# Clustered attention: the stacks are transposed by DMAs from SBUF to SBUF instead of PE and ACT, the softmax shift is one f16 part made on ACT, and the cluster sums are halved twice on POOL

## What is computed

```
x  = layernorm(inputs)
q, k, v = x @ Wq, x @ Wk, x @ Wv                       # per head 8 features
qb = softmax(q @ Whq);  kb = softmax(k @ Whk)          # per head 32 clusters
logits = q @ k.T / sqrt(8) + 0.1 * (qb @ kb.T)
out = (softmax(logits) @ v) @ Wo
```

## Time and profile before

| | |
|---|---|
| median of 3 runs | 1725.93 us (1725.49 to 1727.14) |
| profiled execution | 1726.9 us, its span 1725.1 us |
| PE busy in the span | 1432.3 us (83%) |
| DVE busy | 1264.7 us (73%) |
| ACT busy | 971.7 us (56%) |
| POOL busy | 859.6 us (50%) |
| row maxima on DVE, L656 | 256 x 1216 ns = 311.4 us |
| exponentials on ACT, L703 | 256 x 1028 ns = 263.2 us |
| copies of the stacks on ACT, L724 | 128 x 1028 ns = 131.2 us |
| transposes of the stacks on PE, L555 | 1024 x 228 ns = 83.4 us |

### The profile page before, as it was taken

One profiled execution on the slowest core, in us unless ns is written; L12 is line 12 of the kernel. 1 busy time (PEld: TensorE's weight loads), 2 busy tenths in 40 slices (PEclk: granted clock), 3 DMA queues, 4 the chain that ended last, 5 costly groups with the idle time before them and its releaser, 6 DMA issues. The chain is left out here.

```text
span 1725.1 us, 28685 instructions
## 1 busy us (share of the span) xinstructions
PE 1432.3 (83%) x10436; PEld 707.8 (41%) x10436; DVE 1264.7 (73%) x2008; ACT 971.7 (56%) x1741; POOL 859.6 (50%) x916
## 2 busy tenths in 40 slices
PE   2589999999999985775799999986958999999596
PEld 0233333333333321453455555552425555555343
DVE  6378888888888873335788888876668888888493
ACT  1457777777787754323566666643245666666322
POOL 0846556556455400111977777740058777777000
PEclk9769999999999999788899999998989999999898
DMA  3000000000000000100111110101010101110001
GB/s 88 1 1 2 2 1 2 2 2 1 2 1 2 2 2 9 40 1 21 29 23 23 23 23 23 24 10 40 0 35 23 23 23 23 23 23 23 1 1 51
DMA packets 26495, 27.84 MB, mean 16 GB/s; under 512 B 4682, under 2 KB 18164, under 8 KB 26356
## 3 DMA queue, kind: packets, MB, share of 16 engines
q1 hardware_dynamic: 26356, 26.01, 6.1%
HBM read 8.73 MB, written 2.10 MB: 6 GB/s over the span
## 5 line engine op out<-in xcount | busy, mean ns | idle before, releaser
L656 DVE TENSOR_REDUCE row_max<-max_ps 128x2 f32<-128x1024 f32 x256 | 311.4, 1216 | 48.2 <-PE max_ps L516 47.5
L703 ACT ACTIVATE prob<-scores_ps 128x1024 f32<-128x1024 f32 x256 | 263.2, 1028 | 98.7 <-PE scores_ps L498 98.6
L1637 POOL TENSOR_TENSOR la_turned<-la_raw,lw_rot 128x1024 f32<-128x1024 f32 x64 | 155.0, 2421 | 183.2 <-ACT la_raw L1542 156.8
L1294 PE MATMUL la_ring<-lw_wqkv,la_hT 128*128 128x512 f32 x384 | 201.1, 637 | 47.1 <-DVE la_hT L1411 28.1
L1532 ACT ACTIVATE la_prob<-la_s,la_neg_max 128x128 f32<-128x128 f32 x512 | 156.3, 391 | 52.3 <-DVE la_neg_max L1456 52.3
L498 PE MATMUL scores_ps<-stack 128*128 128x512 f16 x512 | 155.6, 386 | 34.0 <-ACT prob L703 32.5
L724 ACT ACTIVATE stack<-bench 128x1024 f16<-128x1024 f16 x128 | 131.2, 1028 | 59.4 <-PE bench L555 59.4
L1644 POOL TENSOR_TENSOR la_turned<-la_turned,la_swapped 128x1024 f32<-128x1024 f32 x64 | 151.2, 2362 | 20.9 <-DVE la_swapped L1438 16.1
L802 POOL TENSOR_TENSOR cl<-cl,cl_inv 128x512 f32<-128x512 f32 x64 | 67.2, 1049 | 141.5 <-DVE cl_inv L624 141.5
L530 PE MATMUL heads_ps<-prob,v_pad 128*32 128x512 f32 x1024 | 136.4, 605 | 1.1 <-ACT prob L703 1.1
L1648 POOL TENSOR_TENSOR la_turned<-la_turned,la_inv 128x1024 f32<-128x1024 f32 x64 | 121.9, 1905 | 5.0
(11 more groups left out here) (159 smaller groups left out, 3094.7 us busy)
## 6 DMA issues: line engine op xcount, KB each, us to landing
la_v_back<-la_v_own SPq DMA_DIRECT2D x112, 130.0 KB, 2.3
X<-in_x SPq DMA_DIRECT2D x8, 256.0 KB, 5.0
stack<-shift_row SPq DMA_DIRECT2D x128, 2.0 KB
out<-X SPq DMA_DIRECT2D x8, 256.0 KB, 2.5
lw_wqkv<-in_wqkv SPq DMA_DIRECT2D x2, 768.0 KB, 5.0
lw_rot<-in_rot SPq DMA_DIRECT2D x2, 512.0 KB, 6.6
lw_w<-in_fw SPq DMA_DIRECT2D x2, 341.0 KB
mlp_w<-in_mlp_w SPq DMA_DIRECT2D x2, 256.0 KB, 2.9
```

Source lines behind the costliest of these rows:

```text
L656: nc.vector.tensor_reduce(row_max[:, grp % 2, w // 2, :, w % 2], max_ps[:], AX.X, ALU.max).then_inc(max_made, 1)
L703: nc.scalar.activation(prob[:, c % 4, 2 * pr:2 * pr + 2, :], scores_ps[:], ACT.Exp, scale=1.0 / LOGIT_SCALE).then_inc(exp_made, 1)
L1294: nc.tensor.matmul(ring_ps[:, r % 2, :], hT[:, b % 2, t * P:(t + 1) * P], wqkv[:, use * INNER:(use + 1) * INNER], start=True, stop=True).t ...
L1637: nc.gpsimd.tensor_tensor(spun, raw[:, T % 2].rearrange("p s (h f) -> p s h f", f=LD), rot[:, T % TPB, :, 0, :].unsqueeze(2).to_broadcast( ...
```

## The change

- `STACKS`, the four bench uses of the stacks, PE's transposes and ACT's `take_stack` go. SP issues `dma_start_transpose` instead (`turn_stack`), from `stack_tok` to `stack`, 128 tokens by 8 heads by 128 values of f16 each, at the steps 12, 14, 16 and 18 in the order k0, q0, k1, q1, and in a slot behind that slot's `place_shift`. Each part has a semaphore of its own. PE's max scores and POOL's `take_share` wait on these.
- The shift is one f16 value in place of two: `shift_tok` and `shift_row` are half as large, two DMAs place a group's shift in place of four. The scaling (`shift_tokens`) and the copy of the turned rows (`shift_rows`) go from DVE to ACT; the subtraction of the second part goes.
- POOL halves the cluster values a second time (16 to 8), and DVE's sum reads 8 values per head in place of 16.
- `scale_input` goes from step -5 to -10 and `xn` from -3 to -8, which puts `xn` in slot 7; `heads_out` comes one slot earlier on PE (slot 1, behind `qkv`) and on DVE (slot 2).

```diff
-FIRST_STEP, LAST_STEP = -5, 18
+FIRST_STEP, LAST_STEP = -10, 18
@@ def streams(n):
-        "heads_out": every(n - UNITS - 3, UNITS, B * 4),
+        "heads_out": every(n - UNITS - 2, UNITS, B * 4),
@@ def bench_uses(n):
-    for uses, step, at in ((first, "stack_k1", 16), (first, "stack_q1", 18), (first, "stack_k0", 12),
-                           (first, "stack_q0", 15), (first, "xn", -3),
-                           (rest, "qkv", 2), (rest, "clk", 4), (rest, "clq", 6)):
+    for uses, step, at in ((first, "xn", -8), (rest, "qkv", 2), (rest, "clk", 4), (rest, "clq", 6)):
-                          (rest, "heads_out", every(n - UNITS - 2, UNITS, B * 4)),
+                          (rest, "heads_out", every(n - UNITS - 1, UNITS, B * 4)),
-STACKS = ("stack_k0", "stack_q0", "stack_k1", "stack_q1")
+STACK_PARTS = ((1, 0), (0, 0), (1, 1), (0, 1))
...
+        cl_quarter = sb("cl_quarter", [P, 2, H, NB // 4])
-        shift_tok = sb("shift_tok", [P, TPB, 2, 4], F16)
-        shift_row = sb("shift_row", [8, S], F16)
+        shift_tok = sb("shift_tok", [P, TPB, 4], F16)
+        shift_row = sb("shift_row", [4, S], F16)
...
-        stack_made = sem("stack_made")
+        stack_made = {(side, half): sem(f"stack_made_{side}{half}") for side, half in STACK_PARTS}
@@ PE: def make_scores(u):
-                    pe.wait_ge(shift_placed, 64 * (u // UNITS + 1))
+                    pe.wait_ge(shift_placed, 32 * (u // UNITS + 1))
@@ PE: def make_max_scores(u):
                 if g == 0 and w == 0:
-                    pe.wait_ge(stack_made, stacks_made(last, "stack_k0"))
+                    pe.wait_ge(stack_made[1, 0], 16 * (last + 1))
+                    pe.wait_ge(stack_made[0, 0], 16 * last)
                 elif g == 0 and qt == 3:
-                    pe.wait_ge(stack_made, stacks_made(last, "stack_q0"))
+                    pe.wait_ge(stack_made[0, 0], 16 * (last + 1))
                 elif g == 2 and w == 0:
-                    pe.wait_ge(stack_made, stacks_made(last, "stack_q1"))
+                    pe.wait_ge(stack_made[1, 1], 16 * (last + 1))
+                    pe.wait_ge(stack_made[0, 1], 16 * (last + 1))
@@ PE: def fill_bench(use):
-                elif step[:5] == "stack":
-                    side, half = int(step[6] == "k"), int(step[7])
-                    pe.wait_ge(lo_made, turn_of(x, side) + 1)
-                    for i in range(8):
-                        mm = nc.tensor.transpose(bench16[:, i * P:(i + 1) * P],
-                                                 stack_tok[:, side, 8 * half + i, :], ident16[:])
@@ DVE: def cluster_sum(x, side):
-                dve.wait_ge(cl_half_made, c + 1)
-                nc.vector.tensor_reduce(cl_sum[:, side, :], cl_half[:, side], AX.X,
+                dve.wait_ge(cl_quarter_made, c + 1)
+                nc.vector.tensor_reduce(cl_sum[:, side, :], cl_quarter[:, side], AX.X,
...
@@ ACT
-            def take_stack(step, x):
...
+            def shift_tokens(grp):
+                act.wait_ge(max_made, UNITS * (grp + 1))
+                if grp > 0:
+                    act.wait_ge(shift_row_made, grp)
+                nc.scalar.activation(shift_tok[:], row_max[:, grp % 2].rearrange("p q e j -> p q (e j)"), ACT.Copy,
+                                     scale=1.0 / SHIFT).then_inc(shift_made, 1)
+
+            def shift_rows(x):
+                bench = filled("shift", x)
+                if x > 0:
+                    act.wait_ge(shift_placed, 32 * x)
+                nc.scalar.activation(shift_row[:], bench.bitcast(F16)[0:4, 0:S], ACT.Copy).then_inc(shift_row_made, 1)
@@ ACT: def slot(n): behind exponentiate
-                for step, x in first:
-                    if step[:5] == "stack":
-                        take_stack(step, x)
+                if s["shift"] is not None:
+                    shift_rows(s["shift"])
@@ ACT: def slot(n): at the end
+                if s["max"] is not None and s["max"] % UNITS == UNITS - 1:
+                    shift_tokens(s["max"] // UNITS)
@@ POOL: def halve(x, side):
+                half = cl_half[:, side]
+                pool.wait_ge(cl_half_made, c + 1)
+                nc.gpsimd.tensor_tensor(cl_quarter[:, side], half[:, :, 0:NB // 4], half[:, :, NB // 4:NB // 2],
+                                        ALU.add).then_inc(cl_quarter_made, 1)
@@ POOL: def take_share(x, side):
-                    pool.wait_ge(stack_made, stacks_made(x - 1, ("stack_q1", "stack_k1")[side]))
+                    pool.wait_ge(stack_made[side, 0], 16 * x)
+                    pool.wait_ge(stack_made[side, 1], 16 * x)
@@ POOL: def slot(n):
-                if tile_at_step(n, -5) is not None:
-                    scale_input(tile_at_step(n, -5))
+                if tile_at_step(n, -10) is not None:
+                    scale_input(tile_at_step(n, -10))
@@ SP
+            def place_shift(g):
+                sp.wait_ge(shift_row_made, g + 1)
+                for e in range(2):
+                    row, h = FEATURES[e] + 3 * DH, 4 * (g % 4) + e
+                    sp.dma_start(stack[row:row + 1, g // 4 % 2, 0, h:h + 3:2, :],
+                                 shift_row[2 * e:2 * e + 2, :]).then_inc(shift_placed, 16)
+
+            def turn_stack(x, side, half):
+                b, t = x // TPB, x % TPB
+                sp.wait_ge(lo_made, turn_of(x, side) + 1)
+                if t == 0 and b >= 2:
+                    sp.wait_ge(scored, SLOTS * (b - 2) + 16 * (half + 1))
+                sp.dma_start_transpose(stack[:, b % 2, side, 8 * half:8 * half + 8, t * P:(t + 1) * P],
+                                       stack_tok[:, side, 8 * half:8 * half + 8, :].rearrange("p h c -> p (h c)")
+                                       ).then_inc(stack_made[side, half], 16)
+
+            def slot(n):
+                if streams(n)["shift"] is not None:
+                    place_shift(streams(n)["shift"])
+                for step, (side, half) in zip((12, 14, 16, 18), STACK_PARTS):
+                    if tile_at_step(n, step) is not None:
+                        turn_stack(tile_at_step(n, step), side, half)
```

More of the change, by code:

```diff
@@ L460, in clustered_attention @@
         block = ctx.enter_context(nc.Block())
-        def stacks_made(tile, step):
-            return 4 * tile + STACKS.index(step) + 1
         @block.tensor
@@ L676, in slot @@
                         task(tile_at_step(n, step), side)
-                if s["shift"] is not None:
-                    shift_rows(s["shift"])
                 if s["heads_out"] is not None:
@@ L835, in _ @@
         def _(sp):
-            def slot(n):
-                g = streams(n)["shift"]
-                if g is not None:
-                    sp.wait_ge(shift_row_made, g + 1)
-                    heads = slice(4 * (g % 4), 4 * (g % 4) + 4)
-                    for part in range(2):
-                        for e in range(2):
-                            row, src = FEATURES[e] + 3 * DH + part, 4 * part + 2 * e
-                            sp.dma_start(stack[row:row + 1, g // 4 % 2, 0, heads.start + e:heads.stop:2, :],
-                                         shift_row[src:src + 2, :]).then_inc(shift_placed, 16)
+            def place_shift(g):
[12 more added lines that the diff above has]
+                                       ).then_inc(stack_made[side, half], 16)
+            def slot(n):
+                if streams(n)["shift"] is not None:
[3 more added lines that the diff above has]
+                        turn_stack(tile_at_step(n, step), side, half)
             over_slots(slot)
```

35 lines of the change are left out of this document (4 added, 31 removed).

## The result

| | before | after |
|---|---|---|
| median of the runs | 1726.54 us (4 runs) | 1705.01 us (4 runs, 1703.88 to 1706.73) |
| ratio | | 0.9876, 95% interval 0.9859 to 0.9893 |
| profiled execution | 1726.9 us, span 1725.1 | 1705.32 us, span 1703.5 |

The change makes the kernel 21.5 us faster. The forecast was 1718, 8 us faster: its direction and its range held, its size was too small by far.

The account below looks back on a forecast made before the run. PE's 93% was held to overstate its bound: only jobs in odd-to-even intervals count. From 1726.9 us, 13 less for about 26 periods (18.00 to 17.5 us) plus 5 in ramp-up gave 1718.9, median 1718; range 1700 to 1800.

Parts of the forecast that it names:

- part 1: Stacks leave PE and ACT: three of four transpose sets per tile worth nothing, the fourth 0.55 us between slots 5 and 6.
- part 2: Jobs moved between PE's slots: the heads transpose becomes exposed, +0.53 us a period; the xn transpose becomes hidden, -0.26.
- part 3: Shift leaves DVE for ACT: PE's 0.26 us wait for DVE goes; slot 6's late row maximum costs 0 to +0.3.
- part 4: POOL's extra addition, 0.43 us per side and tile: room in the steady part, +3.4 us in ramp-up.
- part 5: Transposing DMAs on SP's queue: k1 lands 0.3 us late, within the 0.7 DVE bears; +4 us in ramp-up.
- T: Time one transposing DMA occupies SP's queue, taken as 2.0 us from the packets of the loads at the start.
- L: The rest of a transposing DMA's time up to its landing, taken as about 1.5 us.
- The condition: For POOL to get k1 in time, 2T + L must stay below 5.9 us; the forecast's values gave 5.5.
- Rival (a): Transposes land too late, so POOL, DVE and PE wait: 28% for 1730 to 1800 us, 10% beyond.
- (b): PE is the bound after all, as its 93% suggests; half of 83.4 us comes back: near 1690 us, 8%.
- (c): The exposed heads transpose and DVE's lateness eat the gain: 17.8 us a period, 1726 us, 12%.
- (d): Ramp-up gets longer because PE, with less to do, keeps the low clock one more period: 1730 us, 4%.

Follow-up runs that it names:

- e1: The kernel before with only PE's stack transposes and ACT's stack copies replaced by transposing DMAs; 1710.07 us, ratio 0.9903.
- e2: The changed kernel with heads_out moved back to the even slot on PE (slot 2; DVE slot 3); 1697.53 us, ratio 0.9836.
- e3: The kernel before with only the one-part shift on ACT and the second halving on POOL, stacks staying on PE and ACT; 1718.25 us, ratio 0.9957.
- e7: e2 without the second halving on POOL, DVE summing 16 values per head again; 1695.61 us, ratio 0.9828.
- e4: The changed kernel with a second transposing DMA of the same source into a spare buffer ahead of each; 1803.87 us, ratio 1.0457.
- e8: e2 with twelve more useless f16 transposes per slot on PE during ramp-up; 1707.42 us, ratio 0.9905.
- e12: The changed kernel with one DVE memset put ahead of the MLP's statistics; 1714.5 us, one execution.

## Why the prediction was wrong, point by point

- **Removing the stacks from PE and ACT, part 1.** The mechanism was right: the even-to-odd intervals stayed at 1.72 to 1.81 in e1 and in the changed kernel. The size was too small. The 0.1 us that ACT's copies had added to S0 to S1 was left out on purpose, and came back (1.82 to 1.72); S1 to S2 gave 0.09 more than its term (2.94 for 3.03), S5 to S6 0.07 (2.71 for 2.78). S6 to S7 stood in the sum as 1.75 though the earlier trace rows has 1.81, and it is still 1.81.
- **The moved jobs, part 2.** heads_out was put at +0.53, the changed kernel has +0.44 and e2 takes 0.39 a period back on the mean: right in kind, 0.1 too high. xn was put at -0.26, and S3 to S4 fell by 0.26. Right.
- **The shift, part 3.** ACT's operations take 0.22 and 0.57 us where 0.3 and 0.5 were taken; e3 gives 0.34 us in 13 periods and 0.76 in six, 0.35 on the mean, where 0.26 stood for all. But e1 shows that most of this goes with the stacks alone, so the cause was put down to the wrong part. The late row maximum of slot 6 was given up to 0.3 us, 0.1 in the value taken; S7 to S0 rose by 0.07.
- **The period.** The terms' own range was 17.4 to 17.7, the value taken 17.5, the trace has 17.24. This is the first failed step, a term mis-sized: 13 us stood in the sum, 19.1 were measured. Two things make the difference. A plain period gave 0.62 us, not 0.5. And the walk took one plain tile for all 26: that even-to-odd intervals are always 1.72 to 1.82 is not so in the kernel before, where S4 to S5 is 2.48 in the six periods with a batch's work, and those gave 1.24 us each. The extra 0.62 in six periods is 3.7 us, more than half of the missing 6.1.
- **POOL, part 4.** One addition costs 0.45 us (0.43 was taken). In ramp-up e7 against e2 puts the halving at 3.7 us (3.4 was taken).
- **The DMAs, part 5.** T was taken as 2.0 and is 1.24, L as 1.5 and is 2.0; from q0's start to k1's landing it makes 4.5 us by these, and 4.6 to 4.9 in most tiles, not 5.5. The bound by bytes, 1.1, was the nearest for T; the times per packet misled. The condition was put at 5.9, the trace and e4 have 5.0. So both errors were nearly of the same size and cancelled, which is luck: with T = 2.0 POOL would have been half a microsecond late in every period. Rival (a)'s mechanism is shown by e4, with 3.0 us a period for a doubled T where the condition gave 1.1. Its price for a late k0 does not follow from its own terms: at T = 3, 2.6 + T + L is 7.1, and that is 0.9 us behind 6.2, not 1.7. As for the rule of the Trainium skill that was weighed there, "VectorE: DVE Perf Modes", section "The three transpose paths": its 1309 ns for one 128x128 block by the crossbar does not add up block by block; eight blocks in one DMA took 1.24 us of the queue and landed in 3.2.
- **Ramp-up.** +5 was forecast, +4.3 came. The DMAs stood in it with 4: POOL's three waits for them are 3.3 us, and e1, which has them alone, starts 3.6 us later.
- **The sum.** Nothing in it stood for the 1038 us behind the attention: it took them as fixed because their code is. That is the second failed step, a term put at nothing without a word on it, and at 7.3 us the larger one: the change ends the attention 14.3 us earlier, and the rest happened to be shorter from there. With this part as before, the median would be some 1712, between the forecast and the result.
- **The rivals.** (b), PE bound by its busy share, is refuted by e1's intervals and by its median, 1710 where 1700 or less was expected for it. (c), the exposed heads eating the gain, named a true cost (9.8 us in e2) but not enough of it. (d) was not decided by e8.
- **What stays open.** Why the part behind the attention differs in length: it goes with the granted clock there, but what sets that clock's course, and whether the start decides it, is not shown. And what the granted clock of ramp-up costs.

The best of the kernels that were run: the DMAs, the shift on ACT, heads_out where it was, and one halving, which is e7: 1695.6 us, 9.4 below the changed kernel by medians. Its part before the MLP is 14.2 us shorter than the changed kernel's (658.6 for 672.8 us), and the part behind is 4.5 us longer.

## What to carry to other kernels

Where single PSUM tiles tie PE to other engines, list the intervals between their uses before pricing a job that leaves PE: a job under the floor of such a loop is free, one beyond it counts in full, and with two loops of opposite phase (here scores with ACT, max scores with DVE) a job hidden from the one lies on the other. A DMA that replaces compute on two engines is paid at the place where its source is overwritten: take the room from what stands ahead of it in its queue to that overwriting, and compare it with spacing and landing. A walk over one period must be made for each kind of period that there is. And stages behind a change can come out longer or shorter though their code is the same, so a forecast of half a per cent needs a term, or a wider range, for them.

## What the runs showed of the hardware that was not expected

- The same instructions from the MLP on took between 1030.4 and 1038.3 us in the profiles of this study, within 0.3 us in two executions of the kernel before, and 4.0 us longer in the one execution in which their start moved by 5.2 us (e12). The three shortest have a mean granted clock of 0.95 there, all others 0.93 or 0.94.
- A transposing DMA of 256 KB from SBUF to SBUF took 1.24 us of SP's queue, and where nothing held up the next one, that mostly started 1.28 us after it, with 32% of the DMA engines' time in use from 130 to 586 us. No operation got longer by it: the even-to-odd intervals stay at 1.72 us, and DVE's row maximum takes 1219 ns on the mean where it took 1216.
- In the kernel before, the shift's scaling on DVE took 1101 ns on the median and 175 at best, for 16 columns. The view is that of one line's instructions (ns as min/median/max), of the kernel before:

```profile
L664 DVE TENSOR_SCALAR shift_tok<-row_max x32: 175/1101/1145, 101.1 to 656.4; 128x16 f16<-128x16 f32 x32
```

The shortest are the four behind 604 us (0.17 us each), where POOL has nothing left to do. All 28 others end 0.03 us behind the end of POOL's L817 or L819. DVE in order of time, one of them, of the kernel before:

```profile
375.08 1.09 DVE L664 TENSOR_SCALAR shift_tok<-row_max 128x16 f16<-128x16 f32 x1
```

POOL at the same place:

```profile
374.99 1.16 POOL L817 TENSOR_TENSOR stack_tok<-cl,stack_tok 128x512 f16<-128x512 f32 x1
376.10 0.43 POOL L819 TENSOR_TENSOR stack_tok<-qkv,stack_tok 128x128 f16<-128x128 f32 x1
```

The one at 375.08 ends at 376.17 and POOL's subtraction at 376.15. One at 357.41, which takes 0.31 us, ends at 357.72, and POOL's L817 there at 357.70. The length is what is left of POOL's instruction, plus little. Read so, up to 0.9 us of DVE's time per shift was waiting for POOL, and part 3 moved this wait away: on ACT the same scaling takes 216 ns. The Trainium skill, "SBUF — State Buffer", section "SBUF: two separate sides", has the rule: DVE in a two-port mode and POOL hold the shared pair of ports exclusively for a whole instruction. These ends agree with it. Whether the scaling ran in such a mode the trace does not show, and no run was made to test it by itself.
